# A DLRM tower on one Trainium2 core: chunk 0 gathered and turned in two halves of 64 samples

## The chip, the cores and the metric

The kernel runs on one core of one Trainium2 chip. What counts is the device time of one execution in microseconds. The kernel before took 1107.88 us (median of 3 runs, 1106.35 to 1109.63).

## What is computed

512 samples with 32 categorical fields each. The embedding rows (64 floats) of the 32 tables are gathered into `e` [512, 32, 64], and a compressed interaction network of two layers runs on it:

```python
e = stack([tbl_f[ids[:, f]] for f in range(32)], axis=1)       # [B=512, F=32, D=64]
z0 = einsum('bhd,bfd->bhfd', e, e).reshape(B, 32 * 32, D)
y0 = relu(einsum('bcd,oc->bod', z0, w0) + b0)                   # 128 outputs
hidden, direct0 = y0[:, :64], y0[:, 64:]
z1 = einsum('bhd,bfd->bhfd', hidden, e).reshape(B, 64 * 32, D)
y1 = relu(einsum('bcd,oc->bod', z1, w1) + b1)                   # 128 outputs
z = concatenate([direct0, y1], axis=1).sum(-1)                  # [B, 192]
h = concatenate([z, dense_ctx], axis=1)                         # [B, 208]
h = relu(h @ W_top1 + b_top1); h = relu(h @ W_top2 + b_top2); y = h @ W_top3
```

All is float32. Nearly all the work is in the two `einsum` pairs, whose products are made on VectorE and summed over channels on TensorE.

## The kernel before

**Chunks and groups.** The 512 samples are 4 chunks (`NC`) of 128. A group is one chunk's 128 samples times 4 values of d (`ND`), 512 columns (`N`); there are 64 groups (`G`), 16 (`GC`) to a chunk, and group g holds d = 4(g % 16) onwards of chunk g // 16.

**Gathers.** POOL gathers with an indirect DMA per field and chunk (`gather(c, f)`, line 292): 128 rows of 256 bytes, one to a partition, into `emb`. The 32 gathers of chunk 0 come first, in one train, once the indices have landed. The other 96 are strewn over the groups by `gathers(g)`: three in each of the groups 0 to 10, two in each one after, one behind each of the three places at which POOL may subtract.

**From a group's rows to columns.** For each group ACT copies the four d of all fields into `stage` (`stage_x`, line 337; at the first group of a chunk it waits for that chunk's gathers), TensorE transposes it into `pt` (`turn_x`, line 588), ACT copies that to `xf` (`copy_xf`, line 343), and SP stores it five times into `x_dram` (`store_x`, line 227) and reads it back in the arrangements that the products want (`x0`, `xt`, `xd`, `xe`: lines 243, 248, 254, 260). Stages and turns run three groups ahead: `turn_x(g + 3)` stands in group g behind `tail(g + 1)`.

**The units.** A group has five: P (layer 1) and A, C, B, D (layer 2). For each, VectorE multiplies two 128x2048 operands into a slot of `zf` (line 494; five slots). A unit is in one of two modes (`mode(unit)`):

- whole ("F"): TensorE multiplies the four blocks of `zf` in float32 with `wf` (line 606; the trace shows two records for each matmul, 8 to a unit).
- split: ACT rounds `zf` to `zh` (`high`, line 361), POOL (mode "P", line 302) or VectorE (mode "V", line 511) subtracts to get the rest `zl` (`low`), and TensorE runs three sets of four fast matmuls: `main` (lines 612 and 613) needs `zh`, `late` (line 622) needs `zl`.

P and D are always whole. A is whole in odd groups below 11, otherwise split on POOL. C is split on VectorE in even groups below 11 and on POOL in odd ones, and then on VectorE in every third group up to 42. B is split on POOL.

**The order of the work** is written out by hand for each engine. On TensorE a group g is: main A(g), late B(g-1), main P(g+1), tail(g+1) (line 627, one matmul for the diagonal part of layer 1), turn_x(g+3), late A(g), main C, main B, main D, late C. On ACT it is:

```python
high(("A", g)); high_s(g + 1); copy_x0(g + 2); stage_x(g + 3); finish_2(g - 1)
high(("C", g)); copy_xf(g + 3); high(("B", g))
finish_straight(g + 1); finish_dir1(g + 1); finish_swapped(g + 1)
```

On POOL: low A, gathers, low C, gathers, low B, gathers. A slot of `zf` is free once TensorE has used a whole unit, or once the low part of a split one has been made.

**Sums over d.** VectorE adds each group's layer outputs into `acc1` and `acc2` (`add_1`, `add_2`), which alternate between two buffers by chunk, and at the chunk's end sums over its 4 d (`sum_d`, line 540) into `zsum`. After the last group TensorE runs the three top layers.

Of the kernel before, what the change touches and what calls it, by code (L numbers as in the profile page):

```python
# [8 lines left out]
I32 = mybir.dt.int32  # L9
ALU = mybir.AluOpType  # L10
ACT = mybir.ActivationFunctionType
AX_X = mybir.AxisListType.X

P = 128
B, F, D = 512, 32, 64
H = 64
NC = B // P
ND = 4
N = ND * P
G = NC * D // ND  # L20
GC = D // ND
# [13 lines left out]
def mode(unit):  # L35
    name, g = unit
    if name in "PD":
        return "F"
    if g == LAST and name != "A":
        return "F" if name == "B" else "V"  # L40
    if name == "A" and g < 11 and g % 2:
        return "F"
    if name == "C" and g < 11:
        return "P" if g % 2 else "V"
    if name == "C" and g < 43:
        return "V" if g % 3 == 0 else "P"
    return "P"
# [1 line left out]

LATER_GATHERS = [(c, f) for c in range(1, NC) for f in range(F)]


def gathers(g):
    first = min(3 * g, 33) + 2 * max(0, g - 11)
    return LATER_GATHERS[first:first + (3 if g < 11 else 2)]


def period(g):  # L60
# [18 lines left out]
def slot(u):  # L79
    return (NTH[u] - 1) % ZF  # L80


def split_slot(u):
    return (NTH_SPLIT[u] - 1) % ZS
# [14 lines left out]
def dlrm_tower(nc, dense_ctx, ids, tables, W_top1, b_top1, W_top2, b_top2, W_top3, w0, b0, w1, b1,  # L99
               eye, out):  # L100
    with ExitStack() as ctx:
        def sb(name, shape, dt=F32):
            return ctx.enter_context(nc.sbuf_tensor(name, shape, dt))

        def ps(name, shape):
            return ctx.enter_context(nc.psum_tensor(name, shape, F32))

        def sem(name):
            return ctx.enter_context(nc.semaphore(name))

        emb = sb("emb", [P, F, NC, D])
        idx = sb("idx", [P, NC, F], I32)
        wh = sb("wh", [P, len(SPLIT_NAMES), T, P], F32R)
        wl = sb("wl", [P, len(SPLIT_NAMES), T, P], F32R)
        wf = sb("wf", [P, len(WHOLE_NAMES), T, P])
# [2 lines left out]
        ident = sb("ident", [P, P])  # L118
        bias0 = sb("bias0", [P, 1])
        bias1 = sb("bias1", [P, 1])  # L120
        xs = sb("xs", [P, 3 * T + 2, N])
        stage = sb("stage", [P, F, ND])
        xf = sb("xf", [P, P])
        zf = sb("zf", [P, ZF, T, N])
        zh = sb("zh", [P, ZS, T, N], F32R)
# [2 lines left out]
        acc1 = sb("acc1", [P, 2, N])  # L128
        acc2 = sb("acc2", [P, 2, N])
        zsum = sb("zsum", [P, 2, B])  # L130
# [37 lines left out]
        pt = ps("pt", [P, N])  # L168
# [6 lines left out]
        x_dram = nc.dram_tensor("x_dram", [G, REPEATS * F, N], F32, kind="Internal")  # L175

        ids_in, consts_in, cin_in, top_in = sem("ids_in"), sem("consts_in"), sem("cin_in"), sem("top_in")
        gathered = [sem("gathered%d" % c) for c in range(NC)]
        w_doubled, w_turned = sem("w_doubled"), sem("w_turned")
        w_high, w_low, s_low, dense_turned = sem("w_high"), sem("w_low"), sem("s_low"), sem("dense_turned")  # L180
        staged, turned, xf_ready, x_stored = sem("staged"), sem("turned"), sem("xf_ready"), sem("x_stored")
# [8 lines left out]
        acc1_done, acc2_done = sem("acc1_done"), sem("acc2_done")  # L190
        zsum_ready = sem("zsum_ready")
# [14 lines left out]
        @block.sync  # L206
        def _(sp):
            sp.dma_start(idx[:], ids.rearrange("(c p) f -> p c f", p=P)).then_inc(ids_in, 16)
            sp.dma_start(ident[:], eye).then_inc(consts_in, 16)
            sp.dma_start(w0_twice[:, 0:1024], w0).then_inc(cin_in, 16)  # L210
            sp.dma_start(w0_twice[:, 1024:2048], w0).then_inc(cin_in, 16)
# [74 lines left out]

        @block.gpsimd
        def _(pool):
            pool.wait_ge(ids_in, 16)

            def gather(c, f):
                pool.indirect_dma_start(  # L292
                    out=emb[:, f, c, :], out_offset=None, in_=tables[f],
                    in_offset=bass.IndirectOffsetOnAxis(ap=idx[:, c, f:f + 1], axis=0),
                ).then_inc(gathered[c], 16)

            def low(u):
                if mode(u) != "P":
                    return
                s, q = slot(u), split_slot(u)  # L300
                pool.wait_ge(hi, NTH_SPLIT[u])
                pool.tensor_tensor(zl[:, q], zf[:, s], zh[:, q].bitcast(F32), ALU.subtract).then_inc(lo["P"], 1)  # L302

            for f in range(F):
                gather(0, f)
            for g in range(G):
                now = gathers(g)
                low(("A", g))
                for c, f in now[0:1]:
                    gather(c, f)  # L310
                low(("C", g))
                for c, f in now[1:2]:
                    gather(c, f)
                low(("B", g))
                for c, f in now[2:3]:
                    gather(c, f)

        @block.scalar
        def _(act):
# [11 lines left out]
            def stage_x(k):  # L331
                if k >= 1:
                    act.wait_ge(turned, k)
                if k % GC == 0:
                    act.wait_ge(gathered[k // GC], 16 * F)
                cols = emb[:].rearrange("p f c d -> p f (c d)")[:, :, ND * k:ND * k + ND]
                act.activation(stage[:], cols, ACT.Copy).then_inc(staged, 1)  # L337

            def copy_xf(k):
                act.wait_ge(turned, k + 1)  # L340
# [52 lines left out]
            stage_x(0)  # L393
            copy_xf(0)
            stage_x(1)
            copy_x0(0)
            copy_xf(1)
# [37 lines left out]
        def _(dve):  # L435
# [60 lines left out]
            def products_s(k):  # L496
                dve.wait_ge(xt_in, 16 * (k + 1))
                if k >= 1:
                    dve.wait_ge(s_lo, k)
                dve.tensor_tensor(pzS[:], xt, px0[:], ALU.mult).then_inc(s_mult, 1)  # L500

            def low_s(k):
                dve.wait_ge(s_hi, k + 1)
                dve.tensor_tensor(zS[H:P], pzS[H:P], zS[H:P].bitcast(F32), ALU.subtract).then_inc(s_lo, 1)  # L504
# [8 lines left out]
            def add_1(k):  # L513
                dve.wait_ge(dir1_ready, k + 1)
                if k >= 1:
                    dve.wait_ge(acc1_done, k)
                s = acc1[H:P, k // GC % 2]
                if k % GC == 0:
                    if k // GC >= 2:
                        dve.wait_ge(zsum_ready, 2 * (k // GC - 2) + 1)  # L520
                    dve.tensor_copy(s, py1[H:P]).then_inc(acc1_done, 1)
                else:
                    dve.tensor_tensor(s, py1[H:P], s, ALU.add).then_inc(acc1_done, 1)

            def add_2(g):
                dve.wait_ge(dir2_ready, g + 1)
                if g >= 1:
                    dve.wait_ge(acc2_done, g)
                s = acc2[:, g // GC % 2]
                if g % GC == 0:  # L530
                    if g // GC >= 2:
                        dve.wait_ge(zsum_ready, 2 * (g // GC - 2) + 2)
                    dve.tensor_copy(s, py2[:, g % 2]).then_inc(acc2_done, 1)
                else:
                    dve.tensor_tensor(s, py2[:, g % 2], s, ALU.add).then_inc(acc2_done, 1)  # L535

            def sum_d(a, c):
                acc, rows = ((acc1, slice(H, P)), (acc2, slice(0, P)))[a]
                dve.wait_ge((acc1_done, acc2_done)[a], (c + 1) * GC)
                dve.tensor_reduce(zsum[rows, a, P * c:P * c + P], acc[rows, c % 2].rearrange("p (d b) -> p b d", d=ND),  # L540
                                  AX_X, ALU.add).then_inc(zsum_ready, 1)

            products(("P", 0))
# [2 lines left out]
            for g in range(G):  # L546
                products(("A", g))
                add_1(g)
                if g + 1 < G:
                    products(("P", g + 1))  # L550
                    products_s(g + 1)
                products(("C", g))
                if g + 1 < G:
                    low_s(g + 1)
                if g >= 1:
                    add_2(g - 1)
                products(("B", g))
                low(("C", g))
                products(("D", g))

                if g % GC == 1 and g > GC:
                    sum_d(0, g // GC - 1)
                if g % GC == 2 and g > GC:
                    sum_d(1, g // GC - 1)
            sum_d(0, NC - 1)
            add_2(LAST)
            sum_d(1, NC - 1)

        @block.tensor
        def _(pe):  # L570
            pe.wait_ge(consts_in, 48)
            pe.wait_ge(w_doubled, 5 + 8)
            for t in range(T * 5):
                src = sym[:, P * t:P * t + P] if t < T else w1_rot[:, P * (t - T):P * (t - T) + P]
                tr = pe.transpose(banks[t // T][:, P * (t % T):P * (t % T) + P], src, ident[:])
# [4 lines left out]
            for c in range(NC):  # L580
                tr = pe.transpose(px0[0:16, P * c:P * c + P], dense[:, c, :], ident[:])
            tr.then_inc(dense_turned, 1)

            def turn_x(k):
                pe.wait_ge(staged, k + 1)
                if k >= 1:
                    pe.wait_ge(xf_ready, k)
                pe.transpose(pt[:, 0:P], stage[:].rearrange("p f d -> p (f d)"), ident[:]).then_inc(turned, 1)  # L588

            def bank(u):  # L590
                return py1[:] if u[0] == "P" else py2[:, u[1] % 2]
# [67 lines left out]

            pe.wait_ge(xf_ready, G)  # L660
            pe.wait_ge(mult, len(UNITS))
            pe.wait_ge(zsum_ready, 2 * NC - 1)
            for m in range(4):
                top_1_begin(m)
            pe.wait_ge(zsum_ready, 2 * NC)
            for m in range(4):
                top_1_end(m)
            for m in range(2):
# [32 lines left out]
```

## Time and profile before

| | |
|---|---|
| median of 3 runs (range) | 1107.88 us (1106.35 to 1109.63) |
| the profiled execution's own time | 1107.58 us |
| its span in the profile | 1105.8 us |
| mean granted TensorE clock | 0.974 of full |
| busy: PE, DVE, ACT, POOL | 1036.2, 943.5, 738.2, 914.6 us |
| DMA moved | 196.89 MB, mean 178 GB/s |

The profile is of one execution, and its times are microseconds from the start of the span. Engines: PE is TensorE's matmuls, PEld its weight loads, DVE is VectorE, ACT ScalarE, POOL GpSimd, SPq the queue of SyncE, which issues the DMAs. L606 is line 606 of the kernel. The granted clock is the share of TensorE's full clock (2.4 GHz) that it was given; 0.50 is 1.2 GHz. Ends of matmuls are modelled, so starts are the surer figure. A timeline row reads: start, duration, engine, line, operation, output and inputs with their shapes, count, and in brackets the engine's idle time before it with what ended it.

### The profile page before, as it was taken

To read this page: it belongs to the slowest core of one execution; us is meant where nothing else is said; L and a number is where in the kernel's file an instruction comes from. 1 tells how busy PE (TensorE), PEld (TensorE's weight loads), DVE (VectorE), ACT (ScalarE), POOL (GpSimd) and SP (SyncE) were. 2 spreads that over 40 slices of the span, in tenths; PEclk is the share of its full clock that TensorE was granted. 3 is DMA by queue.
4 is the path that set the end of the run, shared out by engine and by line. 5 is a ranking of instruction groups with operands and counts; after the bars stand their busy time and mean duration, and the time that the engine had idled before them with its cause. 6 is when DMAs were issued, how large, how long until landed. Compare 5 with 4: busy or idle time off the path is not lost.

```text
span 1105.8 us, 10714 instructions
## 1 busy us (share of the span) xinstructions
PE 1036.2 (94%) x3501; PEld 651.5 (59%) x3501; DVE 943.5 (85%) x621; ACT 738.2 (67%) x907; POOL 914.6 (83%) x300
## 2 busy tenths in 40 slices
PE   1059999999999999999999999999999999999999
PEld 1025556666666666666666566666666666666652
DVE  3059999999999999999999999999889988889860
ACT  1046656767777677777777677777777777777741
POOL 7526778879899999999999899998988898888950
PEclk9569999999999999999999999999999999999998
DMA  4287777777878778787887788777887778877610
GB/s 134 51 195 192 193 187 184 187 195 189 198 192 202 181 194 208 181 200 188 206 199 183 187 197 209 185 198 185 194 204 184 188 184 199 198 184 189 157 39 0
DMA packets 142073, 196.89 MB, mean 178 GB/s; under 512 B 15857, under 2 KB 57457, under 8 KB 141890
## 3 DMA queue, kind: packets, MB, share of 16 engines
q1 hardware_dynamic: 137922, 192.01, 70.2%
q0 software_dynamic: 4096, 4.20, 1.7%
q8 instruction: 28, 0.46, 0.2%
q14 instruction: 27, 0.22, 0.1%
HBM read 175.18 MB, written 20.97 MB: 177 GB/s over the span
## 4 chain that ended last, share of the span: by engine, by line
PE 87%; POOL 3%; DVE 3%; DMA 3%; issue 2%; ACT 2%; SPq 1%; DVEq 0%; ACTq 0%
PE py L606 39%; PE py L622 15%; PE py L612 15%; PE py L613 14%; POOL emb L292 3%; DVE zf L494 2%; DMA xs<-x_dram 1%; ACT zh L361 1%; PE py L627 1%; DMA x_dram<-xf 1%; PE pt L588 1%; DVE zl L511 1%; SPq L260 0%; PE hid L635 0%; PE py L672 0%
## 5 line engine op out<-in xcount | busy, mean ns | idle before, releaser
L302 POOL TENSOR_TENSOR zl<-zf,zh 128x2048 fp32r<-128x2048 f32 x168 | 771.5, 4609 | 121.4 <-ACT zh L361 120.2
L494 DVE TENSOR_TENSOR zf<-xs,hid 128x2048 f32<-128x2048 f32 x256 | 578.8, 2280 | 58.0 <-ACT hid L376 55.4
L606 PE MATMUL py<-zf,wf 128*128 128x512 f32 x1072 | 485.0, 595 | 6.3 <-DVE zf L494 6.3
L361 ACT ACTIVATE zh<-zf 128x2048 fp32r<-128x2048 f32 x186 | 354.5, 1906 | 12.1 <-DVE zf L494 11.8
L606 PEld LDWEIGHTS py<-zf,wf 128*128 128x128 f32 x1072 | 202.9, 190 | 214.6 <-issue 194.0
L612 PE MATMUL py<-zh,wh 128*128 128x512 f32 x744 | 294.3, 396 | 9.4 <-ACT zh L361 9.4
L613 PE MATMUL py<-zh,wl 128*128 128x512 f32 x744 | 292.5, 393 | 0.0
L622 PE MATMUL py<-zl,wh 128*128 128x512 f32 x744 | 234.5, 437 | 1.0 <-POOL zl L302 1.0
L494 DVE TENSOR_TENSOR zf<-xs,px 128x2048 f32<-128x2048 f32 x64 | 146.4, 2288 | 40.1 <-DMA xs<-x_dram 38.2
L622 PEld LDWEIGHTS py<-zl,wh 128*128 128x128 f32 x744 | 135.6, 189 | 61.1 <-issue 33.5
L612 PEld LDWEIGHTS py<-zh,wh 128*128 128x128 f32 x744 | 140.3, 189 | 47.0 <-ACT zh L361 13.5
L292 POOL DMA_INDIRECT emb<-in_tbl,idx x128 | 143.0, 1117 | 29.9 <-issue 24.5
L613 PEld LDWEIGHTS py<-zh,wl 128*128 128x128 f32 x744 | 140.3, 189 | 30.3
L367 ACT ACTIVATE zS<-pzS 128x512 fp32r<-128x512 f32 x64 | 38.4, 600 | 125.1 <-DVE pzS L500 125.1
L391 ACT ACTIVATE py<-py,bias 128x512 f32<-128x512 f32 x64 | 42.1, 659 | 52.4 <-PE py L622 52.4
L343 ACT ACTIVATE xf<-pt 128x128 f32<-128x128 f32 x64 | 17.8, 278 | 72.1 <-PE pt L588 72.1
L535 DVE TENSOR_TENSOR acc<-py,acc 128x512 f32<-128x512 f32 x60 | 41.5, 692 | 18.1 <-ACT py L391 15.7
L352 ACT ACTIVATE px<-xs 128x512 f32<-128x512 f32 x64 | 38.5, 602 | 23.2 <-DMA xs<-x_dram 21.9
L627 PE MATMUL py<-zS,wS 128*128 128x512 f32 x64 | 51.0, 797 | 0.0
L588 PE MATMUL pt<-ident,stage 128*128 128x128 f32 x64 | 18.0, 281 | 33.0 <-ACT stage L337 33.0
L504 DVE TENSOR_TENSOR zS<-pzS,zS 64x512 fp32r<-64x512 f32 x64 | 44.5, 695 | 2.6 <-ACT zS L367 0.7
L384 ACT ACTIVATE hid<-py,bias 32x512 f32<-32x512 f32 x64 | 41.1, 642 | 7.4 <-DVE zf L494 6.2
(74 smaller groups left out, 450.3 us busy)
## 6 DMA issues: line engine op xcount, KB each, us to landing
xs<-x_dram SPq DMA_DIRECT2D x640, 256.0 KB, 4.4
x_dram<-xf SPq DMA_DIRECT2D x64, 320.0 KB, 3.5
emb<-in_tbl,idx POOLq DMA_INDIRECT x128, 4.1
xs<-in_L_rec_w SPq DMA_DIRECT2D x2, 512.0 KB, 4.7
xs<-in_L_rec_w SPq DMA_DIRECT2D x1, 1024.0 KB, 7.3
wt<-in_W_top SPq DMA_DIRECT2D x1, 512.0 KB, 7.3
wt1b<-in_W_top SPq DMA_DIRECT2D x1, 256.0 KB, 6.5
wt1a<-in_W_top SPq DMA_DIRECT2D x1, 128.0 KB, 6.5
```

Of the source, the lines that this page charges most:

```text
L292: pool.indirect_dma_start(out=emb[:, f, c, :], out_offset=None, in_=tables[f], in_offset=bass.IndirectOffsetOnAxis(ap=idx[:, c, f:f + 1], ...
L302: pool.tensor_tensor(zl[:, q], zf[:, s], zh[:, q].bitcast(F32), ALU.subtract).then_inc(lo["P"], 1)
L361: act.activation(zh[:, q], zf[:, s], ACT.Copy).then_inc(hi, 1)
L391: act.activation(py2[:, g % 2], py2[:, g % 2], ACT.Relu, bias=bias1[:]).then_inc(dir2_ready, 1)
L494: dve.tensor_tensor(zf[:, slot(u)], left, right, ALU.mult).then_inc(mult, 1)
L504: dve.tensor_tensor(zS[H:P], pzS[H:P], zS[H:P].bitcast(F32), ALU.subtract).then_inc(s_lo, 1)
L535: dve.tensor_tensor(s, py2[:, g % 2], s, ALU.add).then_inc(acc2_done, 1)
L606: mm = pe.matmul(y, wf[:, w, h], zf[:, s, h], start=first and h == 0, stop=ends and h == T - 1)
L612: pe.matmul(y, wh[:, w, h], zh[:, q, h], start=first and h == 0, stop=False)
L613: pe.matmul(y, wl[:, w, h], zh[:, q, h], start=False, stop=False)
L622: mm = pe.matmul(y, wh[:, w, h], zl[:, q, h], start=False, stop=ends and h == T - 1)
L627: pe.matmul(py1[:], wS[:], zS[:], start=False, stop=True).then_inc(y1_ready, 1)
```

## The change

The 16 groups of chunk 0 are cut otherwise: groups 0 to 7 hold its first 64 samples times 8 d, groups 8 to 15 the other 64 samples times 8 d. The columns of a group stay 512. The first train gathers 64 rows an instruction (samples 0 to 63, partitions 0 to 63), the 32 gathers of samples 64 to 127 join the strewn ones, which now run 7 to a group in groups 0 to 4, 4 in groups 5 to 12 and 2 from then on. They take their indices from `idx_half`, a second load of those rows of `ids`; POOL waits for both loads. A group of chunk 0 is staged as 64 partitions x 2 x 128 and turned by two transposes of 64 rows. The accumulators change buffers and are summed over d at the end of each half too (8 d by 64 samples). The modes change for groups 0 to 12: A is whole in all of them, C is split on POOL in all of them.

```diff
-    if name == "A" and g < 11 and g % 2:
+    if name == "A" and g < 13:
         return "F"
-    if name == "C" and g < 11:
-        return "P" if g % 2 else "V"
+    if name == "C" and g < 13:
+        return "P"
...
+HB = P // 2
+HALVED = GC
+RUN_ENDS = [GC // 2, GC] + [GC * (c + 1) for c in range(1, NC)]
...
-LATER_GATHERS = [(c, f) for c in range(1, NC) for f in range(F)]
+LATER_GATHERS = [(c, f) for c in range(NC) for f in range(F)]
+PER_PERIOD = [7] * 5 + [4] * 8 + [2] * (G - 13)
...
-    first = min(3 * g, 33) + 2 * max(0, g - 11)
-    return LATER_GATHERS[first:first + (3 if g < 11 else 2)]
+    first = sum(PER_PERIOD[:g])
+    return LATER_GATHERS[first:first + PER_PERIOD[g]]
...
+            sp.dma_start(idx_half[:], ids[HB:P, :]).then_inc(ids_in, 16)
...
-            pool.wait_ge(ids_in, 16)
+            pool.wait_ge(ids_in, 32)
+
+            def gather_half(f, h, index):
+                pool.indirect_dma_start(
+                    out=emb[HB * h:HB * h + HB, f, 0, :], out_offset=None, in_=tables[f],
+                    in_offset=bass.IndirectOffsetOnAxis(ap=index, axis=0),
+                ).then_inc(half_gathered if h else gathered[0], 16)
...
             for f in range(F):
-                gather(0, f)
+                gather_half(f, 0, idx[0:HB, 0, f:f + 1])
             for g in range(G):
                 now = gathers(g)
                 low(("A", g))
-                for c, f in now[0:1]:
+                third = (len(now) + 2) // 3
+                for c, f in now[0:third]:
                     gather(c, f)
...
-                if k % GC == 0:
-                    act.wait_ge(gathered[k // GC], 16 * F)
-                cols = emb[:].rearrange("p f c d -> p f (c d)")[:, :, ND * k:ND * k + ND]
-                act.activation(stage[:], cols, ACT.Copy).then_inc(staged, 1)
+                if k < HALVED:
+                    h, d = k // (GC // 2), 2 * ND * (k % (GC // 2))
+                    if first_of_run(k):
+                        act.wait_ge(half_gathered if h else gathered[0], 16 * F)
+                    rows = slice(HB * h, HB * h + HB)
+                    cols = emb[rows, :, 0, d:d + 2 * ND].rearrange("p f (a d) -> p a f d", a=2)
+                    act.activation(stage[rows], cols, ACT.Copy).then_inc(staged, 1)
...
-                pe.transpose(pt[:, 0:P], stage[:].rearrange("p f d -> p (f d)"), ident[:]).then_inc(turned, 1)
+                if k < HALVED:
+                    rows = slice(HB * (k // (GC // 2)), HB * (k // (GC // 2)) + HB)
+                    for a in range(2):
+                        tr = pe.transpose(pt[:, HB * a:HB * a + HB], stage[rows, a].rearrange("p f d -> p (f d)"), ident[rows, rows])
+                    tr.then_inc(turned, 1)
...
-                if g % GC == 1 and g > GC:
-                    sum_d(0, g // GC - 1)
-                if g % GC == 2 and g > GC:
-                    sum_d(1, g // GC - 1)
-            sum_d(0, NC - 1)
+                if g - 1 in RUN_ENDS:
+                    sum_d(0, run(g) - 1)
+                if g - 2 in RUN_ENDS:
+                    sum_d(1, run(g) - 1)
+            sum_d(0, len(RUN_ENDS) - 1)
```

## Rows read from the trace of the kernel before

**Rows 1.** The chain of waits (start, us, what): first gather, last gather, what follows.
```profile
2.99 1.09 POOL emb L292
...
46.05 2.45 DMA emb<-in_tbl,idx
48.58 0.32 ACT stage L337
```

**Rows 2.** Windows: stretch, its length, busy us of each engine, granted clock, DMA share, GB/s.
```profile
20.00:44.00 24.00, 2.54 (x15) 2.19 (x13) 3.30 (x6) 3.06 (x8) 18.21 (x20) 0.61 0.14 26
```

**Rows 3.** Timeline of the start: an issue on SP, the last preparation on DVE.
```profile
1.26 0.48 SPq L209 DMA_DIRECT2D ident<-in_eye  x1
...
23.93 0.68 DVE L471 COPY denseT<-px 16x512 f32<-16x512 f32 x1
```

**Rows 4.** Timeline of PE: the tail matmuls of groups 1, 2, 13 and 14.
```profile
81.89 0.79 PE L627 MATMUL py<-zS,wS 128*128 128x512 f32 x1
99.46 0.79 PE L627 MATMUL py<-zS,wS 128*128 128x512 f32 x1
...
275.72 0.80 PE L627 MATMUL py<-zS,wS 128*128 128x512 f32 x1
291.42 0.80 PE L627 MATMUL py<-zS,wS 128*128 128x512 f32 x1
```

**Rows 5.** POOL's gathers and subtractions: by line (ns min/median/max), and timeline.
```profile
L292 POOL DMA_INDIRECT emb<-in_tbl,idx x128: 940/958/3062, 3.0 to 743.5; - x128
...
L302 POOL TENSOR_TENSOR zl<-zf,zh x168: 4554/4608/4677, 74.4 to 1061.6; 128x2048 fp32r<-128x2048 f32 x168
...
10.63 3.06 POOL L292 DMA_INDIRECT emb<-in_tbl,idx  x1 [0.30 <-issue]
...
74.38 4.56 POOL L302 TENSOR_TENSOR zl<-zf,zh 128x2048 fp32r<-128x2048 f32 x1 [27.40 <-ACT zh L361]
```

**Rows 6.** The stage copy, by line (ns min/median/max, first and last start).
```profile
L337 ACT ACTIVATE stage<-emb x64: 292/294/309, 48.6 to 1017.9; 128x128 f32<-128x128 f32 x64
```

**Rows 7.** Timeline of PE, groups 5 to 7 (A of 5 and 7 whole, of 6 split).
```profile
161.59 3.60 PE L606 MATMUL py<-zf,wf 128*128 128x512 f32 x8
164.62 0.79 PE L627 MATMUL py<-zS,wS 128*128 128x512 f32 x1
165.25 0.27 PE L588 MATMUL pt<-ident,stage 128*128 128x128 f32 x1
...
167.69 0.51 PE L612 MATMUL py<-zh,wh 128*128 128x512 f32 x1 [0.32 <-ACT zh L361]
...
169.66 3.59 PE L606 MATMUL py<-zf,wf 128*128 128x512 f32 x8
...
174.02 0.39 PE L612 MATMUL py<-zh,wh 128*128 128x512 f32 x1
...
179.80 0.79 PE L627 MATMUL py<-zS,wS 128*128 128x512 f32 x1
...
189.62 3.59 PE L606 MATMUL py<-zf,wf 128*128 128x512 f32 x8
...
193.98 0.59 PE L606 MATMUL py<-zf,wf 128*128 128x512 f32 x1
```

**Rows 8.** Timeline of ACT, group 5: the xf copy and the zh of B.
```profile
165.56 0.28 ACT L343 ACTIVATE xf<-pt 128x128 f32<-128x128 f32 x1 [1.28 <-PE pt L588]
165.73 1.91 ACT L361 ACTIVATE zh<-zf 128x2048 fp32r<-128x2048 f32 x1
```

**Rows 9.** Group 0: timeline of ACT and PE, and one window.
```profile
72.40 1.90 ACT L361 ACTIVATE zh<-zf 128x2048 fp32r<-128x2048 f32 x1
74.35 0.79 PE L612 MATMUL py<-zh,wh 128*128 128x512 f32 x1 [5.85 <-ACT zh L361]
77.93 4.52 PE L606 MATMUL py<-zf,wf 128*128 128x512 f32 x8
...
76.00:78.00 2.00, 2.00 (x6) 1.52 (x6) 2.00 (x3) 0.06 (x1) 2.00 (x1) 0.50 0.53 131
```

More of the change, by code:

```diff
@@ L47, in mode, with run, first_of_run @@
     return "P"
-LATER_GATHERS = [(c, f) for c in range(1, NC) for f in range(F)]
+HB = P // 2
+HALVED = GC
+RUN_ENDS = [GC // 2, GC] + [GC * (c + 1) for c in range(1, NC)]
+def run(g):
+    return next(r for r, e in enumerate(RUN_ENDS) if g < e)
+def first_of_run(g):
+    return g == 0 or g in RUN_ENDS
+LATER_GATHERS = [(c, f) for c in range(NC) for f in range(F)]
+PER_PERIOD = [7] * 5 + [4] * 8 + [2] * (G - 13)
 def gathers(g):
-    first = min(3 * g, 33) + 2 * max(0, g - 11)
-    return LATER_GATHERS[first:first + (3 if g < 11 else 2)]
+    first = sum(PER_PERIOD[:g])
+    return LATER_GATHERS[first:first + PER_PERIOD[g]]
 def period(g):
@@ L112, in dlrm_tower @@
         idx = sb("idx", [P, NC, F], I32)
+        idx_half = sb("idx_half", [HB, F], I32)
         wh = sb("wh", [P, len(SPLIT_NAMES), T, P], F32R)
@@ L121, in dlrm_tower @@
         xs = sb("xs", [P, 3 * T + 2, N])
-        stage = sb("stage", [P, F, ND])
+        stage = sb("stage", [P, 2, F, ND])
         xf = sb("xf", [P, P])
@@ L177, in dlrm_tower @@
         ids_in, consts_in, cin_in, top_in = sem("ids_in"), sem("consts_in"), sem("cin_in"), sem("top_in")
-        gathered = [sem("gathered%d" % c) for c in range(NC)]
+        gathered, half_gathered = [sem("gathered%d" % c) for c in range(NC)], sem("half_gathered")
         w_doubled, w_turned = sem("w_doubled"), sem("w_turned")
@@ L288, in _ @@
         def _(pool):
-            pool.wait_ge(ids_in, 16)
+            pool.wait_ge(ids_in, 32)
[4 more added lines that the diff above has]
+                ).then_inc(half_gathered if h else gathered[0], 16)
             def gather(c, f):
+                if c == 0:
+                    gather_half(f, 1, idx_half[:, f:f + 1])
+                    return
                 pool.indirect_dma_start(
@@ L308, in _ @@
                 low(("A", g))
-                for c, f in now[0:1]:
+                third = (len(now) + 2) // 3
+                for c, f in now[0:third]:
                     gather(c, f)
                 low(("C", g))
-                for c, f in now[1:2]:
+                for c, f in now[third:2 * third]:
                     gather(c, f)
                 low(("B", g))
-                for c, f in now[2:3]:
+                for c, f in now[2 * third:]:
                     gather(c, f)
@@ L333, in stage_x @@
                     act.wait_ge(turned, k)
-                if k % GC == 0:
-                    act.wait_ge(gathered[k // GC], 16 * F)
-                cols = emb[:].rearrange("p f c d -> p f (c d)")[:, :, ND * k:ND * k + ND]
-                act.activation(stage[:], cols, ACT.Copy).then_inc(staged, 1)
+                if k < HALVED:
[5 more added lines that the diff above has]
+                    act.activation(stage[rows], cols, ACT.Copy).then_inc(staged, 1)
+                else:
+                    if first_of_run(k):
+                        act.wait_ge(gathered[k // GC], 16 * F)
+                    cols = emb[:].rearrange("p f c d -> p f (c d)")[:, :, ND * k:ND * k + ND]
+                    act.activation(stage[:, 0], cols, ACT.Copy).then_inc(staged, 1)
             def copy_xf(k):
@@ L516, in add_1 @@
                     dve.wait_ge(acc1_done, k)
[L517 to L520, printed above, removed]
+                s = acc1[H:P, run(k) % 2]
+                if first_of_run(k):
+                    if run(k) >= 2:
+                        dve.wait_ge(zsum_ready, 2 * (run(k) - 2) + 1)
                     dve.tensor_copy(s, py1[H:P]).then_inc(acc1_done, 1)
@@ L528, in add_2 @@
                     dve.wait_ge(acc2_done, g)
[L529 to L532, printed above, removed]
+                s = acc2[:, run(g) % 2]
+                if first_of_run(g):
+                    if run(g) >= 2:
+                        dve.wait_ge(zsum_ready, 2 * (run(g) - 2) + 2)
                     dve.tensor_copy(s, py2[:, g % 2]).then_inc(acc2_done, 1)
@@ L535, in add_2, with sum_d @@
                     dve.tensor_tensor(s, py2[:, g % 2], s, ALU.add).then_inc(acc2_done, 1)
-            def sum_d(a, c):
+            def sum_d(a, r):
                 acc, rows = ((acc1, slice(H, P)), (acc2, slice(0, P)))[a]
-                dve.wait_ge((acc1_done, acc2_done)[a], (c + 1) * GC)
-                dve.tensor_reduce(zsum[rows, a, P * c:P * c + P], acc[rows, c % 2].rearrange("p (d b) -> p b d", d=ND),
+                dve.wait_ge((acc1_done, acc2_done)[a], RUN_ENDS[r])
+                b, b0 = (HB, HB * r) if RUN_ENDS[r] <= HALVED else (P, P * (r - 1))
+                dve.tensor_reduce(zsum[rows, a, b0:b0 + b], acc[rows, r % 2].rearrange("p (d b) -> p b d", b=b),
                                   AX_X, ALU.add).then_inc(zsum_ready, 1)
@@ L559, in _ @@
                 products(("D", g))
-                if g % GC == 1 and g > GC:
-                    sum_d(0, g // GC - 1)
-                if g % GC == 2 and g > GC:
-                    sum_d(1, g // GC - 1)
-            sum_d(0, NC - 1)
+                if g - 1 in RUN_ENDS:
[3 more added lines that the diff above has]
+            sum_d(0, len(RUN_ENDS) - 1)
             add_2(LAST)
-            sum_d(1, NC - 1)
+            sum_d(1, len(RUN_ENDS) - 1)
         @block.tensor
@@ L587, in turn_x @@
                     pe.wait_ge(xf_ready, k)
-                pe.transpose(pt[:, 0:P], stage[:].rearrange("p f d -> p (f d)"), ident[:]).then_inc(turned, 1)
+                if k < HALVED:
[3 more added lines that the diff above has]
+                    tr.then_inc(turned, 1)
+                else:
+                    pe.transpose(pt[:, 0:P], stage[:, 0].rearrange("p f d -> p (f d)"), ident[:]).then_inc(turned, 1)
             def bank(u):
@@ L661, in _ @@
             pe.wait_ge(mult, len(UNITS))
-            pe.wait_ge(zsum_ready, 2 * NC - 1)
+            pe.wait_ge(zsum_ready, 2 * len(RUN_ENDS) - 1)
             for m in range(4):
                 top_1_begin(m)
-            pe.wait_ge(zsum_ready, 2 * NC)
+            pe.wait_ge(zsum_ready, 2 * len(RUN_ENDS))
             for m in range(4):
```

## The prediction

> **What bounds the kernel now.** I read the chain of waits first, for where the end is set before the steady work begins. From 3 us to 47 us it consists of nothing but the 32 gathers of chunk 0 on POOL; the last lands 2.45 us after its start, and only then does ACT stage the first group [rows 1]. The windows view says the same from the side: between 20 and 44 us POOL works 18.2 us of 24, PE 2.5 [rows 2]. The last work of the weight preparation on DVE is the copy at 23.93 us [rows 3], so everything but the gathers is ready by 24.6 us: up to 20 us of the train are bare, and a shorter train moves everything behind it forward one for one, if the later stages are not changed.
>
> Then I read TensorE's timeline, one `tail` matmul (line 627) per group as the clock hand. Behind the start TensorE is the bound. From the tail of group 2 to that of group 13 are 275.72 - 99.46 = 176.26 us, 16.02 a group; the next group, with A, C and B all split, takes 15.70 [rows 4]. So what the change does to the periods 0 to 12 has to be read from TensorE's own order, not from POOL's or DVE's load.
>
> **The train (removes time).** 32 gathers of 128 rows become 32 of 64. One takes 0.94 us (median over all 128 of them 0.958) and 0.30 us lie between two [rows 5]. No row shows a gather of another size. If the 0.94 us grew only with the rows, 64 rows would take 0.47 us and the train would be 32 x 0.47 = 15.0 us shorter; if they were all fixed cost, nothing is saved. A gather of fewer rows of the same kind can't be dearer, so zero is the end on that side. There is one row only, of 128 rows, so neither end is nearer: I take the middle, 0.705 us, 32 x 0.235 = **-7.5 us**. The stretched gathers at 10 to 18 us, as the one of 3.06 us, stand beside DVE copies of the weight preparation [rows 5]; these copies stay, so I leave their extra time in both trains.
>
> The trace has nothing that splits the 0.94 us. The Trainium skill, "DMA: Bandwidth & Descriptors", section "Anatomy of one DMA - SWDGE (gpsimd) path", states that descriptor generation is small and that many descriptors can be emitted before their cost shows. By that rule the train would save about 0 in place of 7.5 us; no row here shows it either way. It speaks against this change and is the second rival below.
>
> **Ahead of the train.** POOL now waits for both index loads. The second is issued behind the first on SP, and such an issue takes 0.48 us [rows 3]: **+0.5 us**. All other loads of SP shift by as much and stay under the train.
>
> **First stage and turns.** Staging 64 rows x 256 in place of 128 x 128 (0.29 us [rows 6]) and two transposes in place of one of 0.27 us [rows 7] lie on the path once in front of the first store: about 0.1 and 0.2 us, **+0.3 us**. In the periods 0 to 12 the second transpose adds some 0.05 us each, since each one has half the columns.
>
> **Periods 0 to 12 (adds time).** A of groups 0, 2, 4, 6, 8, 10, 11, 12 goes from split (12 matmuls) to whole (8 records). Seven records of P fill the 3.03 us from 161.59 to 164.62, 0.43 each; D and late C together take 4.36, which leaves 0.23 for each of the four late matmuls [rows 7]. So a whole unit costs 8 x 0.43 = 3.43 us, a split one 12 x 0.228 = 2.74, its main part 1.83, its late part 0.91. Its 8 zh copies leave ACT and its 8 subtractions (4.6 us each [rows 5]) leave POOL. C of 0, 2, 4, 6, 8, 10 and 12 goes from DVE to POOL. The matmuls alone would be 8 x 0.69 = 5.5 us. But a period with a whole A and split C and B exists today in every odd group, and there I read something more. Between the turn and the main part of B stands only the main part of C (1.83 us), while ACT, in its order, copies xf after the turn (165.56) and only then starts the zh of B (165.73, 1.91 us) [rows 8]. So B starts at 167.69, 0.32 us of shown idle and 3.07 us after the tail [rows 7]. In even groups the late part of A (0.91 us) fills that hole. With every A whole the hole is in every period. I put such a period together from measured pieces [rows 7]: tail to B 3.07 (164.62 to 167.69), B main 1.97 (to 169.66), D and late C 4.36 (to 174.02), a whole A and late B 4.36 (189.62 to 193.98), P to its tail 3.03 (161.59 to 164.62): 16.79, with the turn **16.84 us**. A check: tail to tail 164.62 to 179.80 is 15.18 with a split A; a whole one adds 3.43 - 1.83 = 1.60, which gives 16.78.
>
> From tail 1 to tail 13 are 12 such periods, 202.1 us, against 275.72 - 81.89 = 193.8 us now: +8.3. The period behind (15.70) loses the late part of A(12), 0.91 us, and gets the hole, about 0.5: -0.4. The start of group 0: A(0) needs no zh (1.90 us at 72.40), so it starts about 2.1 us sooner, but TensorE is at half clock there (granted clock 0.50, the 1.2 GHz level; the split one starts at 74.35, P(1) at 77.93 [rows 9]); 8 records of twice 0.43 end at 79.1 in place of 77.9, and as P(1) then runs more at full clock, tail 1 comes +0.6 us. Sum **+8.5 us**.
>
> **What I cost at nothing.** DVE loses 7 subtractions; in the stretch read TensorE waits for ACT alone [rows 7], so nothing is gained by that. POOL in the periods 0 to 4: two subtractions and 7 gathers, 9.2 + 7 x (0.705 + 0.30) = 16.2 us, under 16.8; in 5 to 12, 9.2 + 4 x 1.24 = 14.2. The cover of 0.6 us in the first five is gone once a half gather takes over 0.79 us. The gathers of period 0 ahead of C(0) run where POOL idles 27.4 us today [rows 5]. The second half is complete in period 4 and first wanted in period 5; chunk 1 in period 12, wanted in 13. SP issues the same x stores and loads. Two more sums over d on DVE, of half size, fall in the periods 9 and 10, where it has the freed time.
>
> **Sum.** -7.5 + 0.5 + 0.3 + 8.5 = +1.8 us. The profiled execution took 1107.58 us (span 1105.8, 1.8 outside it), 0.3 us under the median shown; 1107.6 + 1.8 = **1109.4 us**. A measurement of this kernel tells about 0.3% (3.3 us) from no change, so this is "within 0.3%".
>
> **The rivals.**
> - *The gather is cheap with 64 rows* (ends faster). With 0.47 us the train gives 15.0 us and the sum is -5.7: 1102 us. For it: 0.94 us for 128 rows is long for an instruction with only a fixed part. Against: nothing seen. It is faster by over 0.3% from 0.54 us downwards. Chance 0.25.
> - *The gather costs nearly the same with 64 rows* (ends slower). Then the train saves nothing, and the first five periods ask 9.2 + 7 x 1.24 = 17.9 us of POOL against 16.8 of TensorE. The low part of B(0) would be done just as TensorE asks for it, so the 4 periods behind lose 1.1 each, 4 us, which TensorE waits for in the late part of B. +0.8 + 8.5 + 4 = +13: 1121 us. It decides from 0.75 us a gather upwards (slower by over 0.3%); POOL itself binds from 0.79. For it: the fastest of 128 gathers and their median are 0.94 and 0.96 us, though they fetch different rows from tables of 1,000 to 125,000 rows beside very different loads, as a fixed cost would [rows 5]. Chance 0.28. (The rule of the Trainium skill quoted above, "DMA: Bandwidth & Descriptors", would end here.)
> - *The hole ahead of B does not come back*, since ACT is freed of A's zh and DVE of C's subtraction. TensorE would then need 3 x 3.43 + 2 x 2.74 for the units and about 0.5 for tail and turn, 16.3 a period: main phase +2.0 in place of +8.5, sum -4.7: 1103 us. For it: the idle shown is only 0.32 us and a zh that is made a little sooner would end it. Against: the order on ACT puts the xf copy, and so the turn, ahead of B's zh whatever its load. Chance 0.1.
>
> The forecast keeps 0.37. The clock adds its own spread: today TensorE runs its first 5 us of group 0 at half clock; had it none of it, 2.7 us less, and a start at another moment can move that either way.
>
> **Numbers.** Faster 0.31, same 0.38, slower 0.31: the forecast and a part of each neighbour lie within 0.3%. The range goes from the cheap gather (1102, less 1 for the clock) to short of the full second rival: 1101 to 1118.
>
> **What would show it.** The length of one half gather in the train decides first: 0.70 us right, 0.5 or 0.9 a rival. The first stage copy would stand at about 41.5 us (48.6 today). The tails of groups 2 to 13 would stand 16.8 us apart each, with an idle of 0.3 us and more of TensorE ahead of every main part of B, put down to ACT; 16.3 would show the third rival. A wait of TensorE for POOL's zl in the periods 1 to 5 shows the second. From tail 14 on the periods should be the old ones. Wrong altogether would be a wait of ACT's stage copy for the second half of the gathers in period 5, or a second transpose that holds TensorE for much more than 0.1 us.

## The result, and the profile after

The changed kernel took 1120.76 us (median of 4, 1120.37 to 1121.62) against 1107.38 us before (median of 4): ratio 1.0129, 95% interval 1.0114 to 1.0143. It is slower by 13 us; "no change" was forecast. Its profiled execution took 1120.41 us, 12.8 more than that of before.

The gathers of the changed kernel by line (ns min/median/max): line 310 has those of 64 rows, first half and second half, line 319 those of 128.
```profile
L310 POOL DMA_INDIRECT emb<-in_tbl,idx x32: 899/903/3102, 3.8 to 45.9; - x32
L310 POOL DMA_INDIRECT emb<-in_tbl,idx_half x32: 900/903/907, 47.1 to 155.7; - x32
L319 POOL DMA_INDIRECT emb<-in_tbl,idx x96: 940/958/2618, 156.9 to 768.5; - x96
```
Half the rows save 0.04 us of 0.94 [rows 5], not the 0.235 of the forecast. The train starts 0.85 us later (3.84 against 2.99 [rows 1]), when the second index load has landed, and its last gather starts at 45.9 us against 46.05, so from first to last start it is 1.0 us shorter. Timeline of the changed kernel, the start of the train and the first stage copy:
```profile
3.84 1.04 POOL L310 DMA_INDIRECT emb<-in_tbl,idx  x1 [3.39 <-DMA idx_half<-in_ids]
...
48.33 0.42 ACT L368 ACTIVATE stage<-emb 64x256 f32<-64x256 f32 x1 [24.70 <-DMA emb<-in_tbl,idx]
```
The stage copy stands at 48.33 us, 0.25 us earlier than at 48.58 [rows 1].

Timeline of PE in the changed kernel, tails of groups 1, 2, 6, 7 and 13, and what stands between two of them:
```profile
80.14 0.50 PE L670 MATMUL py<-zS,wS 128*128 128x512 f32 x1
98.16 0.79 PE L670 MATMUL py<-zS,wS 128*128 128x512 f32 x1
...
111.49 1.19 PE L665 MATMUL py<-zl,wh 128*128 128x512 f32 x4 [0.19 <-POOL zl L329]
...
184.82 0.79 PE L670 MATMUL py<-zS,wS 128*128 128x512 f32 x1
185.54 0.34 PE L628 MATMUL pt<-ident,stage 64*128 64x64 f32 x2
185.81 0.50 PE L655 MATMUL py<-zh,wh 128*128 128x512 f32 x1
...
188.05 0.50 PE L655 MATMUL py<-zh,wh 128*128 128x512 f32 x1
...
201.76 0.80 PE L670 MATMUL py<-zS,wS 128*128 128x512 f32 x1
```
The tails of groups 2 to 6 are 17.4 us apart, those of 6 to 13 are 16.95 (184.82 to 201.76). In the first stretch the late part of B waits for POOL's zl, as at 111.49. POOL there needs 17.38 us a period (98.76 to 116.14) and has no idle in it; one period of it, from C's subtraction to the next:
```profile
98.76 4.61 POOL L329 TENSOR_TENSOR zl<-zf,zh 128x2048 fp32r<-128x2048 f32 x1
103.53 0.91 POOL L310 DMA_INDIRECT emb<-in_tbl,idx_half  x1 [0.16 <-issue]
...
106.88 4.56 POOL L329 TENSOR_TENSOR zl<-zf,zh 128x2048 fp32r<-128x2048 f32 x1
...
116.14 4.62 POOL L329 TENSOR_TENSOR zl<-zf,zh 128x2048 fp32r<-128x2048 f32 x1
```
From group 2 on the main part of B starts 3.23 us after the tail (184.82 to 188.05), and TensorE idles 0.13 us ahead of it, not the 0.3 us and more that the prediction named as its sign. Between tails 1 and 2 it idles longer, 0.45 us ahead of the main part of C and 0.94 ahead of that of B, both for ACT's zh, which waits for DVE's products. What came sooner at tail 1 is given back in part there.

Where the 12.8 us arise, as differences of the tails' starts (after less before):

| stretch | before, us | after, us | difference |
|---|---|---|---|
| start to tail 1 | 81.89 | 80.14 | -1.75 |
| tail 1 to 2 | 17.57 | 18.02 | +0.45 |
| tail 2 to 6 (17.4 a period after) | 65.16 | 69.71 | +4.55 |
| tail 6 to 13 (16.95 a period after) | 111.10 | 118.63 | +7.53 |
| tail 13 to 16 | 46.65 | 47.63 | +0.98 |
| tail 16 to 63 | 730.35 | 729.83 | -0.52 |
| tail 63 to the end | 53.08 | 54.64 | +1.56 |

The last line is the clock. In the top layers TensorE is busy throughout in both kernels, yet is granted half clock for 10.3 us before (windows of 5 us from 1079: 0.93, 0.50, 0.54) and for 13.7 us after (from 1090: 0.80, 0.50, 0.50, 0.83). This length is not a property of the change. It is one of these two in all twelve traces of this document: 10 us also in the runs of experiments 5, 7 and 9, 14 us in the others, among them that of experiment 1, which is the kernel before but for 16 gathers at its start. Windows, first of the kernel before, then of the changed one:
```profile
1084.00:1089.00 5.00, 5.00 (x7) 1.05 (x5) 0.00 (x0) 0.00 (x0) 0.00 (x0) 0.50 0.00 0
```
```profile
1095.00:1100.00 5.00, 5.00 (x6) 1.48 (x6) 0.00 (x0) 0.00 (x0) 0.00 (x0) 0.50 0.00 0
```
In the start the stretch of half clock inside group 0 is 3.4 us after and 6.8 before, worth 1.7 us at the two levels, and tail 0 stands 0.7 us sooner (67.04 against 67.71); the two are more than the -1.75, so the rest, a whole A(0) among it, costs some 0.6 us (an estimate from these numbers). But tail 0 stands anywhere from 65.7 to 68.5 us in the twelve traces, so differences of this size in the start can't be put down to the change.

### The profile page after: what moved, and what is told of

The parts are those of the page before. It is cut to its first block, busy times and chain, and to the rows that moved or that the text cites. A ratio compares the mean times of both kernels' runs of the same rounds, so it can differ in the third digit from the quotient of the medians.

```text
span 1118.6 us, 10694 instructions
## 1 busy us (share of the span) xinstructions
PE 1049.1 (94%) x3485; PEld 644.9 (58%) x3485; DVE 930.9 (83%) x616; ACT 725.9 (65%) x899; POOL 933.3 (83%) x331
## 4 chain that ended last, share of the span: by engine, by line
PE 76%; POOL 10%; issue 5%; ACT 3%; DVE 3%; DMA 2%; SPq 1%; DVEq 0%; ACTq 0%
PE py L649 35%; PE py L665 13%; PE py L655 12%; PE py L656 12%; POOL zl L329 7%; POOL emb L310 2%; ACT zh L397 2%; DVE zf L530 1%; PE py L670 1%; DMA xs<-x_dram 1%; POOL emb L319 1%; DMA xs<-in_L_rec_w 1%; DMA x_dram<-xf 0%; PE pt L631 0%; DVE zl L547 0%
## 5 line engine op out<-in xcount | busy, mean ns | idle before, releaser
L649 PE MATMUL py<-zf,wf 128*128 128x512 f32 x1136 | 513.9, 595 | 9.2 <-DVE zf L530 9.2
L649 PEld LDWEIGHTS py<-zf,wf 128*128 128x128 f32 x1136 | 215.4, 190 | 229.6 <-issue 206.7
L397 ACT ACTIVATE zh<-zf 128x2048 fp32r<-128x2048 f32 x178 | 339.4, 1907 | 11.7 <-DVE zf L530 11.3
L655 PE MATMUL py<-zh,wh 128*128 128x512 f32 x712 | 282.5, 397 | 4.6 <-ACT zh L397 3.1
L656 PE MATMUL py<-zh,wl 128*128 128x512 f32 x712 | 279.0, 392 | 0.0
L665 PE MATMUL py<-zl,wh 128*128 128x512 f32 x712 | 226.6, 440 | 2.5 <-POOL zl L329 2.5
L665 PEld LDWEIGHTS py<-zl,wh 128*128 128x128 f32 x712 | 129.7, 189 | 66.0 <-issue 34.4
L655 PEld LDWEIGHTS py<-zh,wh 128*128 128x128 f32 x712 | 133.7, 188 | 42.9 <-ACT zh L397 10.8
L656 PEld LDWEIGHTS py<-zh,wl 128*128 128x128 f32 x712 | 133.7, 188 | 28.2
L536 DVE TENSOR_TENSOR pzS<-xs,px 128x512 f32<-128x512 f32 x64 | 44.1, 689 | 0.0
```

What stands on the lines that cost most here:

```text
L397: act.activation(zh[:, q], zf[:, s], ACT.Copy).then_inc(hi, 1)
L649: mm = pe.matmul(y, wf[:, w, h], zf[:, s, h], start=first and h == 0, stop=ends and h == T - 1)
L655: pe.matmul(y, wh[:, w, h], zh[:, q, h], start=first and h == 0, stop=False)
L656: pe.matmul(y, wl[:, w, h], zh[:, q, h], start=False, stop=False)
L665: mm = pe.matmul(y, wh[:, w, h], zl[:, q, h], start=False, stop=ends and h == T - 1)
```

## The experiments

Two theories stood after the result. One: a gather is nearly all fixed cost, so the train gives nothing, while the new modes cost some 8 us by the hole ahead of B and POOL's seven gathers some 2 more. The other: the modes cost only their matmuls (5.5 us), and the gathers strewn over the groups are most of the loss. Each ratio below is to the kernel before on the same chip.

**1. What a gather costs by its rows.** Kernel before, and behind its train:
```diff
+            for i in range(16):
+                rows = (96, 64, 32, 16)[i // 4]
+                pool.indirect_dma_start(out=slots[0:rows, i, :], ..., in_=tables[i],
+                    in_offset=bass.IndirectOffsetOnAxis(ap=idx[0:rows, 1, i:i + 1], axis=0))
```


> The kernel before, with 16 further gathers behind the first train, in the time in which POOL idles: four each of 96, 64, 32 and 16 rows, into a tile that is overwritten later. Theory (nearly all of a gather is fixed cost; 128 rows 0.94 us, 64 rows 0.90 us in the changed kernel): 0.92, 0.90, 0.88 and 0.87 us. Rival (the cost falls with the rows once there are few enough): 16 rows at 0.5 us or less. The kernel's time stays at about 1107 us, since POOL has 27 us to spare there.

1108.1 us, a single run. Timeline of its POOL, one of each size (the four of a size agree within 0.02 us):
```profile
45.77 0.92 POOL L310 DMA_INDIRECT zsum<-in_tbl,idx  x1 [0.30 <-issue]
...
50.65 0.90 POOL L310 DMA_INDIRECT zsum<-in_tbl,idx  x1 [0.30 <-issue]
...
55.47 0.86 POOL L310 DMA_INDIRECT zsum<-in_tbl,idx  x1 [0.30 <-issue]
...
61.30 0.85 POOL L310 DMA_INDIRECT zsum<-in_tbl,idx  x1 [0.30 <-issue]
```
96, 64, 32 and 16 rows: 0.92, 0.90, 0.86, 0.85 us. From 16 to 128 rows the gather grows by 0.10 us, 0.9 ns a row, on some 0.83 us that are fixed. The cost follows the number of instructions.

**2. The modes alone,** on the kernel before.
```diff
-    if name == "A" and g < 11 and g % 2:
+    if name == "A" and g < 13:
...
-    if name == "C" and g < 11:
-        return "P" if g % 2 else "V"
+    if name == "C" and g < 13:
+        return "P"
```


> The kernel before with the modes of the change alone (A whole and C split on POOL in groups 0 to 12), gathers and groups as before. Theory (an all-whole-A period costs TensorE its matmuls and the hole ahead of B): tails 16.8 to 16.9 us apart in periods 1 to 12, time +9 to +10, 1117 us. Rival (the modes cost only their matmuls, 8 x 0.69, and the rest of the 13 us is POOL's gathers): 16.3 a period, 1111 to 1113 us.

1114.73 us (1112.37 to 1117.06), ratio 1.0063 (1.0043 to 1.0083). Timeline of its PE:
```profile
164.82 0.79 PE L627 MATMUL py<-zS,wS 128*128 128x512 f32 x1
167.90 0.50 PE L612 MATMUL py<-zh,wh 128*128 128x512 f32 x1 [0.33 <-ACT zh L361]
181.60 0.79 PE L627 MATMUL py<-zS,wS 128*128 128x512 f32 x1
```
16.78 a period, 0.33 us of it idle ahead of B, every time: the hole is back in each period. From tail 1 to tail 13 it loses 7.6 us against before. The median is 2 us better than expected; the theory holds in its period.

**3. The halves alone,** the changed kernel with the modes of before (the diff above, reversed).

> The changed kernel with the modes of before (A whole only in odd groups under 11, C split on VectorE in even ones). Halves, 64-row gathers and their places stay. POOL has two subtractions and seven gathers in each of the first five periods either way, 17.4 us by the changed kernel's trace, so theory: 17.4 a period in the first five, then 16.2; against before +1.2 x 4 or 5 for that, about 0 for the train: 1112 to 1113 us. Rival (what costs is the modes alone): 1108 us.

1118.3 us, ratio 1.0091 (1.0071 to 1.0111), 5 to 6 us more than the theory had. TensorE waits for POOL as said, but a pair of periods takes 36.3 to 36.7 us, not 34.8. Timeline of its DVE and POOL:
```profile
115.46 3.02 DVE L547 TENSOR_TENSOR zl<-zf,zh 128x2048 fp32r<-128x2048 f32 x1
```
```profile
116.47 2.78 POOL L310 DMA_INDIRECT emb<-in_tbl,idx_half  x1 [0.16 <-issue]
```
The one gather of each pair that begins while DVE runs its own subtraction takes 2.78 us in place of 0.90; four subtractions (18.4 us), 14 gathers (12.6), the gaps between them (about 3.5) and that delay (1.9) fill the 36 us of POOL. The delay is not new. The kernel before has 14 such gathers, one in most groups in which DVE subtracts; its DVE and POOL:
```profile
115.71 2.29 DVE L511 TENSOR_TENSOR zl<-zf,zh 128x2048 fp32r<-128x2048 f32 x1
```
```profile
115.85 2.98 POOL L292 DMA_INDIRECT emb<-in_tbl,idx  x1 [0.16 <-issue]
```
The 3.02 us of DVE's subtraction at 115.46 have another ground than the gather: it began while POOL's own subtraction still ran (111.76 to 116.31). That happened twice in this trace; the other 16 subtractions took 2.28 us, gather beside them or not.

The change's C on POOL spares it the delay in groups 0 to 12, so the parts of the change do not add up: 7 us for the modes alone and 10 to 11 for the halves alone make 13 to 14 together. In the stretch in which POOL is so filled, from tail 1 to tail 6, 7.8 us are lost. Another 4.1 us are lost from tail 6 to tail 13, 1.8 of them in the last of these periods, where TensorE waits 1.2 us for POOL's zl; the theory had nothing for that stretch.

**4. The second half gathered early:** 24 of its 32 gathers where POOL idles for 31 us.
```diff
-PER_PERIOD = [7] * 5 + [4] * 8 + [2] * (G - 13)
+EARLY = 24
+PER_PERIOD = [2] * 4 + [3] + [4] * 8 + [2] * (G - 13)
...
+            for c, f in LATER_GATHERS[:EARLY]:
+                gather(c, f)
```


> The changed kernel with 24 of the 32 second-half gathers moved to where POOL idles for 31 us ahead of group 0, so that the first five periods have 2 or 3 gathers, not 7. Theory (POOL's seven gathers bind only the first four periods, 17.4 in place of 16.95 us): -1.8 us against the changed kernel, 1119 us, tails 16.95 apart throughout. Rival (the gathers are most of the loss): 1113 us or less.

1123.4 us, ratio 1.0147 (1.0127 to 1.0166). Its interval overlaps that of the changed kernel (1.0114 to 1.0143), so it is not shown to be slower, but the 1.8 us less that were expected did not come. All periods from tail 2 to 13 are at 16.94, but tails 1 and 2 stand 23.7 us apart (79.43, 103.09). Timeline of its ACT, its SP and its PE there, and one window:
```profile
84.43 0.28 ACT L382 ACTIVATE xf<-pt 128x128 f32<-128x128 f32 x1 [4.51 <-remote]
84.60 1.90 ACT L400 ACTIVATE zh<-zf 128x2048 fp32r<-128x2048 f32 x1
```
```profile
59.69 5.61 SPq L279 DMA_DIRECT2D xs<-x_dram  x4
...
73.00 0.70 SPq L246 DMA_DIRECT2D x_dram<-xf  x1
```
```profile
86.56 0.80 PE L658 MATMUL py<-zh,wh 128*128 128x512 f32 x1 [4.02 <-ACT zh L400]
...
86.00:92.00 6.00, 5.44 (x11) 3.67 (x12) 4.12 (x3) 4.20 (x7) 5.27 (x2) 0.50 0.92 223
```
SP's four issues at 59.69 take 5.61 us (1.86 us in the changed kernel), and the store of group 2 goes out at 73.0 (65.9 there). The xf copy of group 3 waits for that store, B's zh stands behind the copy, and TensorE waits 4.0 us for it. Behind that wait the granted clock is 0.50 from 85.7 to 92.5 us, which costs another 3.4 us at the two levels; the wait and the clock together are the long period. The expectation of experiment 5 takes the gathers beside SP's issues for the cause of the late store. The next trace speaks against gathers alone.

**5. Early gathers, and the xf copy moved behind B's zh.** To number 4:
```diff
                 high(("C", g))
+                high(("B", g))
                 if g + 3 < G:
                     copy_xf(g + 3)
-                high(("B", g))
```


> The kernel with 24 second-half gathers ahead of group 0 (which came out at 1123 us, with one period of 23.7 us at the start), and the xf copy behind B's zh. Theory (the gathers beside the first x loads make SP's issues and the stores late; the xf copy of group 3 waits for the store of group 2, and B's zh stands behind it): the 23.7 us period goes to under 18, the later ones from 16.95 to 16.5: 1123.4 - 6 - 4 = 1113 us. Rival (the late stores themselves hold TensorE): the long period stays, 1119 us.

1115.62 us, ratio 1.0085 (1.0069 to 1.0102), by the ratios 7 us better than number 4 and 2.6 us short of the theory; tails 1 and 2 are 17.97 us apart and the later ones 16.53. But in this trace SP's issues were not slow and the store was not late, with the same 24 gathers beside them. Timeline of its SP:
```profile
62.13 1.87 SPq L279 DMA_DIRECT2D xs<-x_dram  x4
...
67.09 0.44 SPq L246 DMA_DIRECT2D x_dram<-xf  x1
```
So this run doesn't show whether the long period went by the moved copy or because the store left 5.9 us sooner, and why SP was slow in number 4 stays open. What it shows is that gathers beside SP are not enough to slow it. Rows of slow issues, 0.70 us and more each, stand in the traces of experiments 1 and 4, both run on one chip, and for 3 us in that of the changed kernel; number 5 ran on another chip. The later periods, 16.53 in place of 16.94, are the moved copy's doing, as experiments 7 and 8 confirm.

**6. Only six early,** and 6, 6, 5, 5, 5 in the first five periods.

> The changed kernel with 6 second-half gathers behind the train and 6, 6, 5, 5, 5 in the first five periods in place of seven. Theory (POOL binds the first four periods at 17.4 and nothing else there does): 16.95 in all periods from 2 on, -2 to -3 against the changed kernel, 1118 us, the gain kept to the end. Rival (POOL's cover does not matter, or the early six delay the first x loads as the 24 did): 1120 us or more.

1118.67 us, ratio 1.0098 (1.0076 to 1.0119). Every period from tail 2 to 13 is 16.94: the 17.4 are gone. POOL's seven gathers cost 2 us (from tail 1 to tail 13 10.5 us are lost against before, 12.5 in the changed kernel). In this trace tail 1 stands 1.1 us later than in the changed kernel's (81.24 against 80.14), within what the start varies by, and the profiled execution is only 0.7 us shorter; the intervals of the two ratios overlap. The 2 us rest on the periods, not on the total.

**7 and 8. The hole itself:** the move of number 5 on the changed kernel, and on the modes alone.

> The changed kernel with ACT's copy of xf moved behind the zh of B. Theory (the hole ahead of B is ACT waiting for the turn before it may make B's zh): the shown wait of TensorE ahead of B goes, the periods 5 to 12 fall from 16.95 to 16.3 to 16.5 us; the first four stay at 17.4, which is POOL's; about -4 against the changed kernel, 1116 us. Rival (B's zh is late for another reason, or the later xf delays the x loads): no change, 1120 us or more.

> The modes of the change on the kernel before, and the xf copy behind B's zh. Theory: 16.78 a period becomes 16.3 in all twelve, -6 against the modes alone: 1109 us. Rival: 16.78 stays, 1115 us.

1118.95 us, ratio 1.0101 (1.0084 to 1.0119), and 1112.28 us, ratio 1.0036 (1.0021 to 1.0051). Periods fall from 16.95 to 16.53 and from 16.78 to 16.46. B's main part starts 2.94 and 2.75 us after the tail, where it was 3.23 and 3.08. Of the four periods at 17.4 three stay, which are POOL's, and the first is 16.58; the period from tail 1 to 2 is 16.53, not 18.02. On ACT the turn no longer stands ahead of B's zh; what it waits for now is DVE's product of B (timeline of the first of the two):
```profile
183.54 1.92 ACT L397 ACTIVATE zh<-zf 128x2048 fp32r<-128x2048 f32 x1 [1.01 <-DVE zf L530]
```
The mechanism is shown: the hole was ACT's wait for the turn. From tail 1 to tail 13 the two traces are 5.1 and 4.0 us shorter than those without the move. By the ratios 3.1 and 3.0 us reach the time, less than the 4 and 6 expected; from tail 16 to 63 the traces are 1.9 and 1.4 us longer, most of it in single periods, by up to 1.0 us. What makes these longer was not tried.

**9. The way the profile pointed to:** split A in the first groups too, as later ones have it, paid with a few gathers of chunk 1 put where POOL has room. Kernel before with
```diff
-    if name == "A" and g < 11 and g % 2:
-        return "F"
-    if name == "C" and g < 11:
-        return "P" if g % 2 else "V"
...
+EARLY = 3
+PER_PERIOD = [6, 3] + [2] * (G - 2)
...
+            for c, f in LATER_GATHERS[:EARLY]:
+                gather(c, f)
```


> The kernel before with 3 gathers of chunk 1 right behind the train, 6 in group 0, 3 in group 1 and 2 in each later group, which frees POOL for the modes of the later groups (A always split, C split on VectorE in every third) from group 0 on. Theory (what these groups cost beyond 15.5 us is their whole A, the hole and VectorE's subtractions): 15.5 to 15.7 a period from period 2 on, -5 to -7, 1101 to 1103 us. Rival (POOL falls behind at the start and gives it back): 1107 us or more.

1100.37 us (median of 6), ratio 0.9933 (0.9917 to 0.9950): faster than both kernels. Its PE timeline, tails 4 to 5:
```profile
128.81 0.80 PE L630 MATMUL py<-zS,wS 128*128 128x512 f32 x1
144.28 0.80 PE L630 MATMUL py<-zS,wS 128*128 128x512 f32 x1
```
Some 15.5 us a period from tail 4 on; the two ahead of it are 15.96 and 16.50, longer than expected. From tail 1 to tail 13 the trace is 6.1 us shorter than that of before.

**10. Number 9 with the xf copy moved.**

> The same with the xf copy behind B's zh. Theory: where A is split its late part covers the hole, so this changes the time little: within 1 us of the run before it. Rival (the xf copy holds ACT up there too): 1 us or more faster.

1104.76 us (median of 12), ratio 0.9975 (0.9964 to 0.9986): 4 us slower than number 9, a miss of both. Of the 3.0 us between the two profiled spans 1.6 are a longer stretch of half clock at the end and 1.4 longer periods from tail 16 to 63. Between 380 and 900 us ACT's px copy waits 22.4 us for the x loads, 7.3 us in number 9. That fits a store that comes later each period, but was not tried by itself.

## Why the prediction was wrong

- **The step that failed** is the first term, "I take the middle, 0.705 us, 32 x 0.235 = -7.5 us". A half gather takes 0.90 us; the train became 1.0 us shorter and began 0.85 us later (0.5 forecast), and the stage copy came 0.25 us sooner, not 7. These 6.8 us are most of the 11.0 by which the sum missed (+1.8 forecast, +12.8 between the profiled executions). The middle of two ends was no evidence. The rule of the Trainium skill ("DMA: Bandwidth & Descriptors", "Anatomy of one DMA - SWDGE (gpsimd) path": descriptor generation is small) named the right end, and experiment 1 agrees: 0.10 us for 112 rows. It should have had most of the chance, not 0.28; and the range, 1101 to 1118, left out the 1121 us of that rival.
- **The second rival happened** (1121 us forecast for it, 1120.8 measured), though not by its own sum: POOL's excess cost 2 us, not 4 (17.38 us a period against 16.95, where the rival had 17.9 against 16.8: a half gather took 0.90 and not 0.94 us, and behind a subtraction the gap is 0.16 and not 0.30), the second transposes cost more than I had, and the clock took 1.6 us at the end and gave some 1.7 at the start. That the totals agree to 0.3 us is luck.
- **The main phase** was right in kind and near in size: +8.5 forecast. The modes alone cost 7.6 us from tail 1 to 13, at 16.78 a period where the pieces gave 16.79, with the hole ahead of B in each. The third rival (no hole) fell: experiments 7 and 8 show that the order on ACT made the hole, as the prediction had argued. The -0.4 for the period behind came to -0.13 (15.57 against 15.70).
- **The second transpose** was mis-sized: 0.05 us forecast, 0.17 measured (16.95 less 16.78). Tail to the main part of C is 0.99 us (184.82 to 185.81), against 0.66 in group 5 before (164.62 [rows 7] to 165.28): two transposes and two weight loads stand there in place of one each. Of these 0.33 us only 0.17 reach the period, since 0.20 fall into the hole ahead of B, which shrinks from 0.33 to 0.13 us. Over the eleven periods from tail 2 to 13 that is 1.8 us (seen in full in experiment 6).
- **What I cost at nothing** held for DVE, the staging and the second half's due time. For POOL it did not: the prediction itself had the cover gone from 0.79 us a gather, and 0.90 did it.
- Tails 13 to 16 lose 1 us more, with TensorE waiting for POOL's zl (0.6 us shown). I did not test its cause.

## What to carry to other kernels

A gather by indirect DMA costs POOL an instruction (0.83 us and the 0.30 us between two), hardly its rows, up to the 128 tried here: what saves POOL's time is fewer gathers, not smaller ones. Before an engine is relieved by making a unit "whole" elsewhere, look at what the removed piece was covering; here 0.91 us of late matmuls hid ACT's turn-around. And where one row prices a whole change, the middle between two ends is no price. Experiment 1 measured it in one run, in time in which POOL was idle, and could have come first.

## What the runs showed of the hardware

- The gather's duration by rows: 16, 32, 64, 96, 128 rows take 0.85, 0.86, 0.90, 0.92, 0.94 us.
- A gather that begins while DVE subtracts (`zl = zf - zh`, both inputs in SBUF) is held until the subtraction is over, and ends 0.78 to 0.83 us behind it. In the twelve traces 142 of 143 such gathers behave so and take 1.9 to 3.0 us; the one exception began 0.03 us behind the start of the subtraction. Beside DVE's products, which have one input in PSUM, 690 gathers took 0.85 to 0.98 us. The Trainium skill, "SBUF — State Buffer", section "Who interferes with whom", has a DVE instruction with two SBUF inputs contend with a GpSimd instruction that reads SBUF. These rows agree if a gather counts as one that reads SBUF, for its indices, which no run here shows by itself.
- Two DVE subtractions that began while POOL's subtraction was in its last 0.85 us took 3.0 us in place of 2.28 (experiment 3).
- Four DMA issues of SP took 5.61 us in experiment 4 and 1.87 us in experiment 5, with the same gathers beside them. The cause is open.
- TensorE was granted half clock for 10 or 14 us in the top layers of every kernel here, while it was busy all the time. In the kernel before it ran matmuls whose weights have 16 and 64 rows from 1077.9 us, fell to 0.50 at 1083.3, began those of 128 rows at 1088.9 and was back at full clock at 1093.6. The two lengths differ by 3.4 us, which is 1.7 us of time, and either kernel's variants show both.
